# Two heads side by side in 64-row tiles, batch work between the blocks of head pairs

## The reference

```python
x = x + attn_a(ln(x))   # 16 heads of 16, causal, bias -slope_h * |i - j|, biases on q, k, v, out
x = x + ffn(ln(x))      # routed: only the first 1024 of all rows (of 8192) have experts; + bias on all
x = x + attn_b(ln(x))   # 16 heads of 16, causal, rotary positions on q and k, no biases
x = x + ffn(ln(x))
# attention of one head: softmax(q @ k.T / 4 + bias) @ v, exp after the row maximum is taken off
# ffn: each routed row goes to 2 of 8 experts: gelu(row @ w1[e]) @ w2[e], times its weight
```

## Time and profile before

| | |
|---|---|
| median of three runs | 5481.02 us |
| profiled execution, first to last instruction | 5479.5 us |
| around the span (median less span) | 1.5 us |
| PE, DVE, ACT, POOL busy | 90, 65, 58, 11% |
| mean granted clock of TensorE | 0.956 of 2.4 GHz |
| instructions | 115362 |
| moved by DMA | 278.45 MB |

### The profile page before, as it was taken

The page is one execution under the profiler, slowest core; times in us unless marked ns, Lnnn a source line. Parts: engine busy times, 40 slices in busy tenths (PEclk is TensorE's granted clock), DMA queues, the critical chain, the costliest instruction groups (busy, mean ns, idle before and its releaser), DMA issues.

```text
span 5479.5 us, 115362 instructions
## 1 busy us (share of the span) xinstructions
PE 4942.7 (90%) x29820; PEld 2236.2 (41%) x29820; DVE 3575.6 (65%) x9222; ACT 3156.7 (58%) x6661; POOL 584.8 (11%) x1479
## 2 busy tenths in 40 slices
PE   5999899998999899969689998999979998899897
PEld 2333433343333433358433334333433334333376
DVE  5778577857776677730377765778567785777600
ACT  2777566765666466732246772667536674566622
POOL 1000110011000200020210002000110002100101
PEclk9999999999999999989899998999989999999998
DMA  4221121103110311045221101211021111111154
GB/s 110 48 35 22 44 58 35 29 25 71 31 32 8 80 28 35 15 144 182 75 49 25 31 8 41 57 30 25 25 56 29 25 19 42 42 31 25 53 169 142
DMA packets 193432, 278.45 MB, mean 51 GB/s; under 512 B 45000, under 2 KB 155848, under 8 KB 192224
## 3 DMA queue, kind: packets, MB, share of 16 engines
q1 hardware_dynamic: 189664, 261.84, 20.4%
q0 software_dynamic: 3072, 8.39, 0.5%
HBM read 124.59 MB, written 43.25 MB: 31 GB/s over the span
## 4 chain that ended last, share of the span: by engine, by line
PE 73%; issue 11%; DVE 6%; ACT 5%; POOL 2%; DMA 1%; SPq 1%; ACTq 1%; DVEq 0%; another core or an unknown queue 0%; POOLq 0%
PE ps_acc L824 18%; PE ps_s L796 17%; PE ps_m L771 15%; ACT probs L597 3%; PE ps_s L931 3%; PE ps_s L748 3%; PE ps_o L834 3%; PE ps_s L799 2%; PE ps_m L941 2%; PE ps_o L941 2%; PE ps_s L910 2%; DVE ps_m L1048 2%; ACT acc_sb L590 2%; PE ps_acc L748 1%; DVE parts L1119 1%
## 5 line engine op out<-in xcount | busy, mean ns | idle before, releaser
L597 ACT ACTIVATE probs<-ps_s 128x512 f32<-128x512 f32 (+3 forms) x5120 | 2459.2, 538 | 1110.1 <-PE ps_s L796 641.7
L1051 DVE TENSOR_REDUCE part_max<-ps_m 128x1 f32<-128x512 f32 x3072 | 1998.2, 684 | 318.1 <-PE ps_m L771 317.1
L771 PE MATMUL ps_m<-stacks 108*128 108x512 bf16 (+7 forms) x5120 | 1790.0, 354 | 156.7 <-DVE part_max L1051 69.6
L796 PE MATMUL ps_s<-stacks 111*128 111x512 bf16 (+7 forms) x5120 | 1757.3, 356 | 98.5 <-issue 54.6
L1048 DVE CUSTOM_DVE_ANT_0 ps_m<-ps_m,mask 128x128 f32<-128x128 f32 (+3 forms) x2048 | 1002.8, 500 | 491.4 <-PE ps_m L771 482.0
L824 PE MATMUL ps_acc<-probs,v_head 128*32 128x512 f32 (+3 forms) x11264 | 1272.1, 516 | 1.9
L796 PEld LDWEIGHTS ps_s<-stacks 111*128 111x128 bf16 (+1 forms) x5120 | 498.7, 98 | 1362.9 <-ACT probs L597 997.1
L771 PEld LDWEIGHTS ps_m<-stacks 108*128 108x128 bf16 (+1 forms) x5120 | 503.3, 98 | 702.1 <-DVE part_max L1048 229.3
L799 PE MATMUL ps_s<-early,identb 128*128 128x128 bf16 x2048 | 453.7, 222 | 0.0
L824 PEld LDWEIGHTS ps_acc<-probs,v_head 128*32 128x32 f32 x11264 | 315.2, 108 | 333.1 <-issue 145.2
L504 POOL CAST cpart<-negmax 128x8 bf16<-128x8 f32 x256 | 50.8, 198 | 3315.2 <-DVE negmax L1056 3315.2
(11 more groups left out here) (114 smaller groups left out, 3362.7 us busy)
## 6 DMA issues: line engine op xcount, KB each, us to landing
stacks<-parts SPq DMA_DIRECT2D x1536, 64.0 KB
stacks<-w_dram SPq DMA_DIRECT2D x60, 1024.0 KB
stacks<-crow SPq DMA_DIRECT2D x768, 2.0 KB
xn<-x_in_dram SPq DMA_DIRECT2D x4, 2048.0 KB, 15.8
xb<-x_in_dram SPq DMA_DIRECT2D x4, 2048.0 KB, 8.4
x_before_ffn<-xb SPq DMA_DIRECT2D x8, 1024.0 KB, 5.2
x_after_a<-parts SPq DMA_DIRECT2D x4, 2048.0 KB, 10.7
xn<-x_after_a SPq DMA_DIRECT2D x4, 2048.0 KB, 15.0
```

The lines of the kernel that those rows point to most:

```text
L597: act.activation(probs[:, n % 8, 0:QW - q0], ps_s[:, s_bank(j, n)[0], q0:QW], ACT.Exp)\
L771: pe.matmul(ps_m[:, bank, 0:w], q_stack(slot)[0:rows, qb * P:(qb + 1) * P], k_stack(slot)[0:rows, kc * QW:kc * QW + w], start=True, stop=T ...
L796: mm = pe.matmul(ps_s[:, bank, q0:QW], k_stack(slot)[0:rows, kb * P:(kb + 1) * P], q_stack(slot)[0:rows, qt * QW + q0:(qt + 1) * QW], star ...
L1051: dve.reduce_max(part_max[:, qb, kc:kc + 1], ps_m[:, bank, 0:w], AX_X).then_inc(item_used, 1)
```

## The change

The kernel is written anew around a pair of heads; mathematics and FFN stay.

- q and k are cut in two float32r pieces of 12 leading bits (a float32 of which the array takes the leading bits), three products of 16 rows, and with position and maximum rows a head has 54 rows. Two heads lie in one stack, rows 0 to 63 and 64 to 127. `scores` and `unit` issue one matmul per head and half of the array, into two banks. Masks are two bf16 matmuls of 64 columns per head on each diagonal block, in both passes; DVE's masked maximum goes, and one `tensor_reduce` takes both heads.
- Value products: a tile of 32 columns is a head and a half of the 512 queries, so the four tiles need not be summed. ACT evacuates 128x256, SP stores it to DRAM; the division by the sum of exps comes later, on POOL, by batch.
- PSUM: four banks for the maxima, a ring of three banks (`RING`) for scores and all other matmuls, one for the value sums.
- No `Fori`: 64 pairs (two layers in one row) of 40 steps are unrolled. `front(f)` lists the next batch's norm, transposes, projections, rope, splits and stores by step, `back(r)` the previous batch's division, output projection and residual; `JOBS` deals them out to the steps of the eight pairs of the batch between. Every engine runs through the same list.
- q and k pieces, value sums and reciprocals go through DRAM; ACT copies every projection out of PSUM, POOL does rope, split and residual, and the norm's root by Newton steps.
- The first batch's `front` and the last one's `back` stand alone at the ends.

```diff
-SLOTS = 4
-GROUP = 4
-NPART = 6
-Q_PARTS = (0, 0, 0, 1, 1, 2)
-K_PARTS = (0, 1, 2, 0, 1, 0)
-POS = 12
+SLOTS = 3
+RING = 3
+PBUF = 12
+CH = 4
+CW = CH * P
...
+PV_LAG = 5
+LAST_GROUP = {3: 3, 2: 6, 1: 8, 0: 9}
+EVAC_STEP = {3: 18, 2: 30, 1: 38}
+LATE_EVAC = 2
+C_HI, C_LO = 34, 4
+def front(f):
+    out = []
+    for c in range(NQ):
+        at = 60 * c
+        out += [(max(0, at - 38), ("ld", f, c, 0)), (at + 1, ("cs", f, c, 0)), (at + 5, ("ln", f, c, 0)),
+                (at + 11, ("xt", f, c, 0)), (at + 13, ("xt", f, c, 1))]
+        for u in range(4):
+            t = at + 20 + 7 * u
+            out += [(t, ("qk", f, c, u)), (t + 2, ("sw", f, c, u)), (t + 3, ("sp", f, c, u)), (t + 9, ("st", f, c, u))]
+        out += [(at + 48, ("v", f, c, 0)), (at + 55, ("v", f, c, 1))]
+    return out
+def back(r):
+    out = [(8, ("rl", r, 0, 0)), (14, ("rc", r, 0, 0)), (15, ("rs", r, 0, 0))]
+    for c in range(NQ):
+        at = 60 * c
+        out += [(at + 18, ("bl", r, c, 0)), (at + 24, ("bm", r, c, 0)),
+                (at + 31, ("y", r, c, 0)), (at + 33, ("ba", r, c, 0)),
+                (at + 38, ("y", r, c, 1)), (at + 40, ("ba", r, c, 1)), (at + 44, ("bs", r, c, 0))]
+        if routed(r, c):
+            out += [(at + 43, ("fn", r, c, 0))]
+    return out
...
+            def load_stack(g):
+                s, beta, p = g % SLOTS, g // PAIRS, g % PAIRS
+                if p == 0:
+                    for i in range(2):
+                        sp.wait_ge(parts_st[i], 16 * 16 * (beta + 1))
+                if g >= SLOTS:
+                    sp.wait_ge(ring_mm, PLACE[("s", g - SLOTS, STEPS - 1, 1)] + 1)
+                for stack, i, order in ((qs[s], 0, (0, 0, 1)), (ks[s], 1, (0, 1, 0))):
+                    for j, piece in enumerate(order):
+                        src = parts_d[beta % 2, i, piece, 2 * DH * p:2 * DH * (p + 1), :]
+                        load_rows(stack, DH * j, src, stack_in[s])
+                if beta < B:
+                    load_rows(qs[s], POS, table(T_SLOPE + 4 * p, 2), stack_in[s])
+                    load_rows(ks[s], POS + 2, table(T_NEG + 4 * p, 2), stack_in[s])
+                elif g < NG // 2 + SLOTS:
+                    load_rows(qs[s], POS, table(T_ZERO, 4), stack_in[s])
...
+            def store_o(g, qt):
+                e = evac_index(g, qt)
+                beta, p = divmod(g, PAIRS)
+                sp.wait_ge(acc_out, e + 1)
+                for u in range(2):
+                    for hi in range(2):
+                        to = o_d[beta % 2, 2 * p + u, :, qt * QW + hi * D:qt * QW + (hi + 1) * D]
+                        tile = 32 * (2 * u + hi)
+                        sp.dma_start(to, acc_sb[tile:tile + DH + 1, e % 2, :]).then_inc(o_st[e % 2], 16)
...
-            def exp_block(ly, hb, h, j, n, opening):
-                qt, kb, q0 = BLOCK[n]
-                act.wait_ge(s_mm, upto(BLOCKS, ly, hb, h, n + 1))
-                if not opening:
-                    act.wait_ge(pv_mm, upto(GROUPS, ly, hb, h, n // 4 - 1))
-                act.activation(probs[:, n % 8, 0:QW - q0], ps_s[:, s_bank(j, n)[0], q0:QW], ACT.Exp)\
-                    .then_inc(exp_done, 1)
+            def exp_block(g, n):
+                qt, kb, q0 = BLOCK[n]
+                i, at = PLACE[("s", g, n, 0)], STEPS * g + n
+                act.wait_ge(ring_mm, i + 2)
+                if at >= PBUF:
+                    act.wait_ge(pv_mm, (at - PBUF) // 4 + 1)
+                for u in range(2):
+                    act.activation(probs[:, at % PBUF, u, 0:QW - q0], ring(i + u)[:, q0:QW], ACT.Exp)\
+                        .then_inc(ring_used, 1)
+            def acc_evac(g, qt):
+                e = evac_index(g, qt)
+                act.wait_ge(pv_mm, GROUPS * g + LAST_GROUP[qt] + 1)
+                if e >= 2:
+                    act.wait_ge(o_st[e % 2], 64 * (e // 2))
+                act.activation(acc_sb[:, e % 2, :], ps_acc[:, e % 2 * D:(e % 2 + 1) * D], ACT.Copy).then_inc(acc_out, 1)
...
-                mm = pe.matmul(ps_s[:, bank, q0:QW], k_stack(slot)[0:rows, kb * P:(kb + 1) * P],
-                               q_stack(slot)[0:rows, qt * QW + q0:(qt + 1) * QW], start=True, stop=True)
-                if kb >= 4 * qt:
-                    mm = pe.matmul(ps_s[:, bank, q0:q0 + P], identb[:, :], early[:, :], start=False, stop=True,
-                                   skip_group_check=True)
-                mm.then_inc(s_mm, 1)
+            def scores(g, n):
+                qt, kb, q0 = BLOCK[n]
+                i, s = PLACE[("s", g, n, 0)], g % SLOTS
+                if n == 0:
+                    pe.wait_ge(rows_in[1], 32 * (g + 1))
+                if n == FIRST_LO:
+                    pe.wait_ge(rows_in[0], 32 * (g + 1))
+                pe.wait_ge(ring_used, i - 1)
+                mm = [None, None]
+                diagonal = kb >= 4 * qt
+                for u in range(2):
+                    r = slice(HALF * u, HALF * u + ROWS)
+                    mm[u] = pe.matmul(ring(i + u)[:, q0:QW], ks[s][r, kb * P:(kb + 1) * P],
+                                      qs[s][r, qt * QW + q0:(qt + 1) * QW], start=True, stop=True)
+                if diagonal:
+                    for part in range(2):
+                        for u in range(2):
+                            r = slice(HALF * u, HALF * u + HALF)
+                            lo = q0 + HALF * part
+                            mm[u] = pe.matmul(ring(i + u)[:, lo:lo + HALF], mk[r, 2 + part, :], id64[r, :], start=False,
+                                              stop=True, skip_group_check=True)
+                for u in range(2):
+                    mm[u].then_inc(ring_mm, 1)
+            def unit(g, n):
+                qb, kc, w = UNIT[n]
+                at, s = STEPS * g + n, g % SLOTS
+                if n == 0:
+                    pe.wait_ge(stack_in[s], stack_count(g))
+                if at >= 2:
+                    pe.wait_ge(p1_used, at - 1)
+                mm = [None, None]
+                diagonal = kc == qb // 4
+                for u in range(2):
+                    r = slice(HALF * u, HALF * u + MAX)
+                    mm[u] = pe.matmul(ps_p[:, at % 2 * 2 + u, 0:w], qs[s][r, qb * P:(qb + 1) * P],
+                                      ks[s][r, kc * QW:kc * QW + w], start=True, stop=True)
+                if diagonal:
+                    for part in range(2):
+                        for u in range(2):
+                            r = slice(HALF * u, HALF * u + HALF)
+                            lo = w - P + HALF * part
+                            mm[u] = pe.matmul(ps_p[:, at % 2 * 2 + u, lo:lo + HALF], mk[r, part, :], id64[r, :],
+                                              start=False, stop=True, skip_group_check=True)
+                for u in range(2):
+                    mm[u].then_inc(p1_mm, 1)
+            def times_v(g, grp):
+                beta, p = divmod(g, PAIRS)
+                pe.wait_ge(ring_used, PLACE[("s", g, 4 * grp + 3, 1)] + 1)
+                for n in range(4 * grp, 4 * grp + 4):
+                    qt, kb, q0 = BLOCK[n]
+                    e, at = evac_index(g, qt), STEPS * g + n
+                    if kb == 0 and e:
+                        pe.wait_ge(acc_out, e)
+                    for u in range(2):
+                        for hi in range(2):
+                            lo, to = max(q0, D * hi), D * (hi + 1)
+                            if lo >= to:
+                                continue
+                            tile = 32 * (2 * u + hi)
+                            first = e % 2 * D + lo - D * hi
+                            mm = pe.matmul(ps_acc[tile:tile + DH + 1, first:e % 2 * D + D],
+                                           v_head[:, beta % 2, kb, 2 * p + u, :], probs[:, at % PBUF, u, lo - q0:to - q0],
+                                           start=kb == 0, stop=kb == 4 * qt + 2 * hi + 1, skip_group_check=True)
+                mm.then_inc(pv_mm, 1)
...
+            for g in range(NG):
+                for n in range(STEPS):
+                    scores(g, n)
+                    if g + 1 < NG:
+                        unit(g + 1, n)
+                    for j in JOBS[g][n]:
+                        job(*j)
+                    if n >= PV_LAG and (n - PV_LAG) % 4 == 0:
+                        times_v(g, (n - PV_LAG) // 4)
+                    if n + STEPS == 4 * (GROUPS - 1) + PV_LAG and g % (NG // 2):
+                        times_v(g - 1, GROUPS - 1)
+                if g % (NG // 2) == NG // 2 - 1:
+                    times_v(g, GROUPS - 1)
+                    if g == NG - 1:
+                        for j in AFTER:
+                            job(*j)
+                    experts(g // (NG // 2))
...
-                    dve.tensor_tensor_reduce(ps_m[:, bank, 0:w], ps_m[:, bank, 0:w], mask[:, QW - w:QW], 1.0, LOWEST,
-                                             ALU.add, ALU.max, part_max[:, qb, kc:kc + 1]).then_inc(item_used, 1)
-                else:
```

(3 more changed lines are left out.)

1482 lines of the change are left out of this document (648 added, 834 removed).

## The result

The changed kernel takes 5732.27 us (median of four runs, 5713.13 to 5737.64) against 5481.41 beside it (four runs, 5472.98 to 5486.33): ratio 1.046, 95% interval 1.0438 to 1.0483. The forecast was 5037 us. The profiled execution has a span of 5711.3 us.

A forecast was written before the change was run, and what follows sets the result against it. TensorE, busy 90%, was taken as the bound. Start 185, first batch 524, 48 pairs 3216, last batch 482, its output 78 and FFN 550 gave 5035, with 1.5 around the span 5037 us; eight-in-ten range 4550 to 5720.

The forecast's parts named there:

- the sum: Whole kernel: start, first batch, 48 pairs of heads, last batch, its output and FFN add to 5035 us.
- Pair matmul, 0.22: Scores of two heads: 54-row float32r matmuls side by side in two array halves take 0.22 us per 512-column pair.
- The forecast's test for this: Profile after: two score records of one step within 0.05 us, next matmuls 0.22 later, showing pair and rate.
- plain step: Two-head step without value products: 1.12 us, of which PE works 0.44; over 1.3 would mean type or pairing wrong.
- value step: Step holding the value products: 0.44 plus 0.22 for switches plus 1.72, 2.38 us, with ScalarE having only two exps.
- Rival (1): Score pair: halves in turn or float32r at half rate, 0.44 a pair, +1.04 a group, 5700 us; chance 0.17.
- Value group, 1.72 + 0.22: Value products of four steps: 32 records in 1.72 us by array time, plus 0.22 for both switches.
- rivals (2): Value products bound by issue at 77 ns a record: 2.46 us a group, 5510 us in all, slower; chance 0.08.
- (2b): Value products: issue binds half way, 0.065 us a record, 2.1 us a group, 5274 us in all; chance 0.08.
- the forecast's 67.0: A pair of heads: 56.5 us of steps plus evacuations, maxima, jobs, transposes, LayerNorm and late stores, 67.0 us.
- Rival (4): Between pairs: trips through DRAM are late, 3 us of waiting a pair, 5229 us in all; chance 0.10.
- rival (3): Steps: less coupling, PE and VectorE work set the pace, 50 us a pair, 3950 us; half way 4490; chance 0.11.

The follow-up runs named there:

- fill: Changed kernel with the two row-maxima unit matmuls issued twice in plain steps without a projection job: 5419.89 us, ratio 0.9893 to the kernel before.
- late: Changed kernel with transposes of normalized rows 4 steps later and the output projection 7 steps later: 5679.36 us, ratio 1.0395 to the kernel before.
- pv1: Changed kernel with value products of one block issued in each step instead of four blocks in every fourth: 4950.25 us, ratio 0.9063 to the kernel before.
- pv1late: pv1 and late joined, on the changed kernel: 4816.92 us, ratio 0.8796 to the kernel before.
- spread: pv1late with the output side's jobs 68 steps apart for each quarter batch instead of 60: 4814.93 us, ratio 0.8805 to the kernel before.
- rates: Changed kernel with runs of back-to-back matmuls of several types and tilings added behind the last FFN, TensorE alone: 5720.78 us.
- rates2: Changed kernel with float32r pairs behind the last FFN, with waits, signals, alternating stacks and value products between: two pairs plus 16 value records 1.65 us.

## Why the prediction was wrong

**The sum by its parts.** The part ahead of the first pair took 198.58 us (forecast 185). The stretch with the FFN took 343.03, of which one pair is 72: 271 (forecast 275). What follows the start of the last pair took 459 (413), with 87 us of waits for GpSimd in it. These make some 60 us; nearly all the rest of the 676 us that the span lies over the sum are the 62 pairs, 10.0 us each.

**Pair matmul, 0.22: right as a rate, wrong as it was used.** The earlier trace rows and the type's argument held: float32r side by side has 0.234 a pair in a run of them. But the step hangs on a latency. The forecast's test for this had two parts. Two score records within 0.05 us: met, they start 3 or 4 ns apart. Next matmuls after 0.22: failed, the unit pair comes 0.34 behind the scores, and the exps start 0.57 behind them instead of 0.43. The 0.43 was read from bf16 blocks, and it holds there even where the block had waited for an exp (1010.96 in the earlier trace rows); in the kernel before:

```profile
1010.97 0.39 PE L796 MATMUL ps_s<-stacks 111*128 111x512 bf16 x1
1011.19 0.38 PE L771 MATMUL ps_m<-stacks 108*128 108x512 bf16 x1
1011.39 0.60 ACT L597 ACTIVATE probs<-ps_s 128x512 f32<-128x512 f32 x1 [0.50 <-PE ps_s L796]
```

There the next matmul comes 0.22 to 0.23 behind and the exp 0.43 (by the trace's ns). The float32r pair is 0.11 and 0.14 later. What fits is its weight load, 0.19 for a pair of records against 0.10, which behind idle time lies under no earlier matmul; it was not tested by itself. With 0.65 from the exp's start to the next scores (forecast 0.67) the plain step is 1.22, not 1.12; the unit pair starts 0.33 behind the scores, and the value products 0.33 behind it, so the value step is 2.52, not 2.38. A group of four steps is 3 x 1.21 + 2.52 = 6.15 against 5.74: 4.1 us a pair, some 260 in all. Rival (1) named that place with a price of 1.04 a group for another reason; 0.41 came, and neither turns nor half rate. That the measured time lies near its 5700 is luck.

**Value group, 1.72 + 0.22: right.** 1.85 us for the group at full clock; 32 records at 0.057 are 1.83. So rivals (2) and (2b), issue, are out, and so is the forecast of 5203 from 0.062 a record. Groups over 2 us, which the forecast had as a sign of issue, there are, but at the lower clock.

**The clock: the step that the sum did not have.** Every duration of the pairs was taken from rows at a clock of .98, and the change was forecast to leave TensorE at work 0.44 of each 1.12 us in plain steps, with no question asked what the clock would do. It fell to 1.2 GHz in part of the value groups, which cost 3.5 to 3.6 us there, unhidden. Over all groups of the trace, from the first value record to the next matmul, this makes 334 us over a full clock (1.85 for 32 records, 1.64 for 24), 5.2 a pair; in fill it makes 119. The window at 1323.03 and fill show the price: 71.8 us at .79, 63.4 at .95. Fill gave 312 us back, net of its own work, and that is 4.9 us a pair. With 4.1 of latency and the 0.8 that late took away, 9.8 of the 10.0 are named; that the three add up was not tested, and so close a sum is partly luck. What is shown is that more matmuls in idle time raise the clock and shorten the kernel. How much an unchanged program would take at full clock throughout was not measured.

**Jobs and trips.** The pair at 1173.98, with jobs at a clock of .98, took 72.2: the forecast's 67.0 and 4.1 make 71.1, so in this pair jobs and side terms were sized to about 1 us. Rival (4), late trips through DRAM, had 3 us a pair: TensorE's waits for GpSimd between the pairs make 0.9, the longest 8.5 us, and late took them all away. Other pairs take up to 92 us, and late has some of 80 to 88 without these waits; what lengthens them is open.

**Coupling, rival (3), was in the program's order.** The sum took the value step as given: 2.38 us, with ScalarE having two exps to do. Its own numbers, 3.7 of TensorE's work a group against 4 x 1.12, said that value products spread over the steps would fit in the wait for the exps. pv1 does that, and its pairs of 51.3 us, those without jobs, are the 50 us of rival (3). As that rival was put it was wrong for this kernel. The change itself, heads side by side, is not what loses: with the same matmuls in another order it is 12% faster than the kernel before (pv1late), with spread the best version that was run.

## What to carry to other kernels

Count a small matmul in a loop by its latency to the consumer and by its rate apart, and put independent TensorE work in single portions into the wait of each step, not in a lump behind four. Before durations are carried from a trace to a changed kernel, ask how idle TensorE becomes: a change that takes work from it can lower its clock and cost more than the work; repeating a matmul in idle time is a cheap test of that.

## What the runs showed of the hardware

- float32r with 54 rows in two row tiles: 0.234 us for a pair of 512 columns in a run (rates), 0.34 to the next pair when it stands behind idle time (1202.45 in the kernel after) or behind column tiles (rates2); with 128 rows 0.23 a matmul inside the run, where float32 takes 0.86.
- The two matmuls of such a pair start 3 or 4 ns apart in the kernel after; in the back-to-back runs of rates up to 50 ns.
- A change between 64-row tiles and 32-column tiles and back costs 0.28 us in rates2, some 0.1 of it the longer first pair.
- In a pair of row tiles the exp that waits for the first half starts 0.59 us after the pair's start, no earlier than one that waits for both (0.57).
- A wait that is already met and a signal on each matmul cost nothing measurable in a run of pairs.
- With the clock at 0.50 the value group takes 3.55 us for 1.85. It fell there in a program whose TensorE is busy 81% of the span on the page; in the kernel before, with 90%, the mean clock is .956, and in pv1 with 88% it is .930.
